# Two half-chunk chains, interleaved, for the feed-forward that runs behind the attention

## What is computed

```python
x = x + attention(layernorm(x), ctx)                 # 16 heads, softmax over 1601 columns
n = layernorm(x)                                     # "t1"
logits = n @ router_w.T                              # "router"
w, top1 = softmax(logits).max(-1), logits.argmax(-1)
x = x + w * (n @ expert_w[top1].T + expert_b[top1])  # "e0".."e15", then the bias, "gb"
n = layernorm(x)                                     # "t2"
a = softmax(where(mask, -1e9, n @ win_k)) * gauss    # "score"
x = x + tanh(concat(a @ ctx, n) @ W_c.T)             # "aT", "z"
n = layernorm(x)                                     # "t3"
h = gelu(n @ w1 + b)                                 # "h"
alpha = softmax_of_top8((h @ w2) / tau)              # "logits", one row of 64 slots per token
slots = (alpha.T @ n) / alpha.sum(0)                 # "slots"; GRU and attention on 64 slots
x = x + alpha @ f(slots)                             # "alphaT", at the very end
```

## The kernel before

| step | before |
| --- | --- |
| turn attention output, y | 10, 12; 15, 17 |
| t1, router | 28, 30; 33 |
| e0 to e15 | 38, 42, 48, 52, 58, 64, 68, 72, 76, 80, 84, 88, 92, 98, 102, 106 |
| gateT; gb | 55; 112, 114 |
| t2, score | 125, 127; 130, 132 |
| aT, z | 145, 147; 150, 158 |
| t3, h, logits, slots, alphaT | 178, 180; 183; 189; 203; 207 |

## Time and profile before

### The profile page before, as it was taken

How to read it: one execution, slowest core, us unless ns; L and a number is a source line. 1 busy time by engine, 2 the same in 40 slices (tenths; PEclk the granted TensorE clock), 3 DMA queues, 4 the chain that set the end, 5 groups by cost and what they waited for, 6 DMA issues and landing times.

```text
span 1084.4 us, 13614 instructions
## 1 busy us (share of the span) xinstructions
PE 978.2 (90%) x4794; PEld 390.6 (36%) x4794; DVE 745.5 (69%) x1704; ACT 571.3 (53%) x1063; POOL 63.8 (6%) x91
## 2 busy tenths in 40 slices
PE   6799999999889999989889989989989999889986
PEld 3453323323333334423323333423333333334643
DVE  4688888887677777776677777776767764235634
ACT  2456766666454456665445546665445547740330
POOL 3441000000000000000000000000000000100000
PEclk9899999999899989999899989999899989999999
DMA  7936500001000000001000000001000000140022
GB/s 187 200 73 111 121 1 15 16 1 35 1 16 1 16 1 14 3 1 55 1 16 1 15 1 13 3 1 54 1 15 1 0 2 1 40 125 2 1 97 78
DMA packets 33931, 36.19 MB, mean 33 GB/s; under 512 B 6670, under 2 KB 30523, under 8 KB 33603
## 3 DMA queue, kind: packets, MB, share of 16 engines
q1 hardware_dynamic: 32542, 34.17, 12.5%
q10 hardware_dynamic: 1242, 0.90, 0.6%
q0 software_dynamic: 80, 0.26, 0.1%
HBM read 21.55 MB, written 7.35 MB: 27 GB/s over the span
## 4 chain that ended last, share of the span: by engine, by line
issue 51%; PE 30%; DVE 9%; DMA 2%; ACT 2%; POOL 2%; DVEq 2%; SPq 1%; POOLq 0%; ACTq 0%
PE ps_m L1064 7%; PE ps_o L1148 7%; PE ps_e L1350 5%; DVE mx L1651 4%; PE ps_e L1022 2%; DMA xres<-in_x 1%; PE ps_m L1350 1%; SPq L545 1%; PE ps_m L1168 1%; PE ps_m L1298 1%; POOL rstd L684 1%; POOL xres L735 1%; PE ps_m L1301 1%; DVE xn L1643 1%; DMA x<-xres 1%
## 5 line engine op out<-in xcount | busy, mean ns | idle before, releaser
L1651 DVE TENSOR_REDUCE mx<-ps_m 128x1 f32<-128x401 f32 x1024 | 538.3, 568 | 198.0 <-PE ps_m L1064 190.6
L848 ACT ACTIVATE probs<-ps_e 128x512 f32<-128x512 f32 (+1 forms) x763 | 437.1, 598 | 342.2 <-PE ps_e L1350 340.5
L1064 PE MATMUL ps_m<-k_stack,q_stack 99*128 99x401 bf16 x1024 | 319.4, 343 | 36.6 <-DVE mx L1651 34.9
L1350 PE MATMUL ps_e<-q_stack,k_stack 101*128 101x512 bf16 (+1 forms) x763 | 299.5, 394 | 10.9 <-ACT probs L848 8.7
L1148 PE MATMUL ps_o<-probs,v_heads 128*32 128x512 f32 (+1 forms) x1664 | 228.9, 623 | 0.0
L1350 PEld LDWEIGHTS ps_e<-q_stack,k_stack 101*128 101x128 bf16 (+1 forms) x763 | 75.9, 100 | 261.8 <-ACT probs L848 167.7
L1064 PEld LDWEIGHTS ps_m<-k_stack,q_stack 99*128 99x128 bf16 x1024 | 102.0, 100 | 183.8 <-DVE mx L1651 131.0
L1252 PE MATMUL ps_m<-expert_w,xnT 128*128 128x512 f32 x192 | 99.4, 598 | 15.2 <-DVE xb L1788 15.2
L1148 PEld LDWEIGHTS ps_o<-probs,v_heads 128*32 128x32 f32 (+1 forms) x1664 | 33.1, 109 | 60.7 <-issue 49.4
L848 ACT ACTIVATE probs<-ps_m 128x512 f32<-128x512 f32 (+1 forms) x69 | 41.6, 603 | 15.2 <-PE ps_m L1350 15.1
L1788 DVE SCALAR_TENSOR_TENSOR xb<-ps_m,hot,xb 128x256 f32<-128x256 f32 x84 | 40.6, 484 | 7.9
(11 more groups left out here) (333 smaller groups left out, 720.0 us busy)
## 6 DMA issues: line engine op xcount, KB each, us to landing
q_stack<-q_parts SPq DMA_DIRECT2D x78, 64.0 KB, 2.6
expert_w<-in_expert_wT SPq DMA_DIRECT2D x2, 1024.0 KB, 12.9
xres<-in_x SPq DMA_DIRECT2D x4, 512.0 KB, 3.8
x<-xres SPq DMA_DIRECT2D x4, 512.0 KB, 3.2
probs<-x SPq DMA_DIRECT2D x1, 2048.0 KB, 8.5
k_stack<-alphaT SPq DMA_DIRECT2D x10, 200.1 KB, 7.6
probs<-in_ctxT SPq DMA_DIRECT2D x3, 512.0 KB, 7.5
q_parts<-probs SPq DMA_DIRECT2D x4, 384.0 KB, 3.0
```

The lines of the kernel that those rows point to most:

```text
L848: act.activation(probs[0:n, k % 2, h, :], score_bank(c, k, h)[0:n, :], ACT.Exp).then_inc(s["exp_done"], 1)
L1064: pe.matmul(ps_m[:, (UNITS * n1 + u) % RING, 0:SPLIT], qst[0:MAX_ROW, g, h, P * t:P * t + P], kst[0:MAX_ROW, HG * g + h, QUARTER_START[q]: ...
L1350: pe.matmul(score_bank(c, k, h)[0:n, :], kst[0:ROWS, HG * g + h, P * st:P * st + n], qst[0:ROWS, g, h, :], start=True, stop=True).then_inc ...
L1651: dve.tensor_reduce(mx[:, q, col:col + 1], ps_m[:, (UNITS * n1 + u) % RING, 0:SPLIT], AX.X, ALU.max)\
```

## The change

Behind chunks 1 to 3, the feed-forward of a chunk runs as two chains, one for tiles 0 and 1, one for tiles 2 and 3. `HALF_STEPS` is placed once for each, with the second chain's first step 6 quarters after the first one's router, and its first expert at least 5 quarters after the first chain's last. Both chains and the row-maxima and output jobs share the same two banks. From the hidden layer on (`h`, `logits`, `slots`, `alphaT`) the chunk stays whole (`choice`). Each engine goes on with three generators in turn in every quarter.

- A job of a half has both 128-row blocks in one bank: `turned_half` writes two k by two tiles, ScalarE takes them with one copy. The number of copies stays 10 a chunk. The weights' transpose goes to `attT`, not `aT`.
- An expert job is the same tile by two experts, but in four products of 256 columns in quarters AT to AT + 3, where it was two of 512.
- Router, gate, softmax and root steps are done by halves: the same element count in twice as many instructions. There are semaphores for each half.
- Normalised tiles are due 1 quarter ahead of the transposes (3 or 4 before); expert jobs of a chain start at least 5 quarters apart (4 before).
- `z` starts with the products that don't need the transposed weights.
- The last chunk's feed-forward keeps its order and uses the same functions, run through `at_once`; so its experts too are in 256 columns.

```diff
-JOBS = [("ota", None, 10, 3), ("otb", "ota", 2, 3), ("y0", "otb", 3, 3), ("y1", "y0", 2, 3), ("t1a", "y1", 11, 3),
-        ("t1b", "t1a", 2, 3), ("router", "t1b", 3, 2), ("e0", "router", 5, 6)]
-JOBS += [(f"e{i}", f"e{i - 1}", 4, 6) for i in range(1, 4)] + [("gateT", "e3", 3, 3), ("e4", "gateT", 1, 6)]
...
+HALF_STEPS = [("ot", None, 10, 3), ("y", "ot", 3, 3), ("t1", "y", 8, 3), ("router", "t1", 3, 2), ("e0", "router", 5, 6),
+              ("e1", "e0", 5, 6), ("gateT", "e1", 2, 3)]
+HALF_STEPS += [(f"e{i}", f"e{i - 1}", 5, 6) for i in range(2, NE // 2)]
+HALF_STEPS += [("gb", f"e{NE // 2 - 1}", 4, 4), ("t2", "gb", 9, 3), ("score", "t2", 3, 3), ("aT", "score", 9, 3), ("z", "aT", 3, 9), ("t3", "z", 15, 3)]
+LAST_STEPS = [("h", "t3", 3, 5), ("logits", "h", 6, 2), ("slots", "logits", 14, 6), ("alphaT", "slots", 4, 3)]
...
+        if name == "ot" and h:
+            return at.get(("router", 0), NEVER) + 6
+        if name == "e0" and h:
+            return max(at.get((f"e{NE // 2 - 1}", 0), NEVER) + 5, at.get((after, h), NEVER) + lag)
...
+def go_on(works, quarter):
+
+    for work in works:
+        while work[1] <= quarter:
+            work[1] = next(work[0], NEVER)
...
-                    for k in range(KT):
-                        yield AT[name] + 2 * k
-                        mm = pe.matmul(bank(name, c), xnT[:, k, P * t:P * t + P], expert_w[:, k, CT * j:CT * j + CT],
-                                       start=(k == 0), stop=(k == KT - 1))
...
+                for e in range(2):
+                    for k in range(KT):
+                        if e or k:
+                            yield AT[f"e{i}", h] + 2 * e + k
+                        mm = pe.matmul(half_bank(f"e{i}", c, h)[:, D * e:D * e + D], xnT[:, k, tok:tok + P],
+                                       expert_w[:, k, CT * j + D * e:CT * j + D * e + D], start=(k == 0), stop=(k == KT - 1))
...
-                yield AT["t1a"] - 4
-                normal(xa, NC + 3 * c + 1)
...
+                yield AT["t1", h] - 1
+                normal_half(xa, 0, c, h)
...
+                work = [begin(steps) for steps in (behind(c - 1, 0), behind(c - 1, 1), choice(c - 1))] if c else []
```

More of the change, by code:

```diff
@@ L193, in begin, with at_once @@
     return [steps, next(steps)]
-def go_on(work, quarter):
-    while work and work[1] <= quarter:
-        work[1] = next(work[0], NEVER)
+def go_on(works, quarter):
+    for work in works:
+        while work[1] <= quarter:
+            work[1] = next(work[0], NEVER)
+def at_once(steps):
+    for _ in steps:
+        pass
 JOB = job_numbers()
@@ L730, in _, with rsqrt_half @@
             pool.wait_ge(s["hb_ready"], 1)
-            def behind(c):
+            def rsqrt_half(i, c, h):
+                pool.wait_ge(var_half[h], 3 * c + i + 1)
+                pool.tensor_tensor(var_e[:, tiles(h)], mv[:, tiles(h), 1], eps[:, tiles(h)], ALU.add)
+                pool.drain()
+                pool.tensor_tensor(rstd[:, tiles(h)], var_e[:, tiles(h)], neg_half[:, tiles(h)], ALU.pow).then_inc(rstd_half[h], 1)
+            for c in range(NC):
                 pool.wait_ge(s["x_loaded"], 16 * (c + 1))
@@ L886, in behind, with window_exp @@
+            def window_exp(c, h):
+                act.wait_ge(negmax_half[h], c + 1)
+                act.activation(tail[:, tiles(h)], st4[:, 0, tiles(h)], ACT.Exp, bias=neg_big[:, 0:1])
+                for t in range(HT * h, HT * h + HT):
                     last = act.activation(work2[:, t, :], work[:, t, :], ACT.Exp, bias=st4[:, 0, t:t + 1],
                                           accum_out=rowsum[:, t:t + 1])
-                last.then_inc(s["rowsum_ready"], 1)
-                yield AT["aTa"] + 2
@@ new lines, in norm_turned, with rows_half @@
+            def norm_turned(i, c, h):
+                pe.wait_ge(xn_half[h], 3 * c + i + 1)
+                yield from turned_half(f"t{i + 1}", c, h, xn)
+            def rows_half(name, c, h, after, rows, weights):
+                wait_half_taken(pe, after, c, h)
+                half_free(pe, name, c, h)
+                for t in range(HT):
+                    if t:
+                        yield AT[name, h] + t
+                    for k in range(KT):
+                        mm = pe.matmul(half_bank(name, c, h)[:, D * t:D * t + D], rows[:, k, HC * h + P * t:HC * h + P * t + P],
+                                       weights[:, k, :], start=(k == 0), stop=(k == KT - 1))
+                fills_half(mm, name, c, h)
@@ L1219, in behind @@
+            def behind(c, h):
+                yield AT["ot", h]
+                if c == 0 and h == 0:
                     pe.wait_ge(s["ld_fill"], N_FILL)
@@ new lines, in behind @@
+                router_half(c, h)
+                for i in range(NE // 2):
+                    yield AT[f"e{i}", h]
+                    yield from expert_half(i, c, h)
+                    if i == 1:
+                        yield AT["gateT", h]
+                        gates_half(c, h)
+                yield AT["gb", h]
+                yield from bias_half(c, h)
+                yield AT["t2", h]
+                yield from norm_turned(1, c, h)
+                yield AT["score", h]
+                yield from rows_half("score", c, h, "t2", xnT, win_k)
@@ L1740, in behind @@
[L1740 to L1755 removed]
+                last.then_inc(var_half[h], 1)
@@ L1822, in behind @@
[L1822 to L1830 removed]
+                last.then_inc(a_half[h], 1)
```

951 lines of the change are left out of this document (396 added, 555 removed).

## The result

The changed kernel takes 1119.03 us, median of 4 runs (1117.1 to 1124.97), against 1087.07 (1086.31 to 1095.68) for the kernel before on the same chip: ratio 1.0285, 95% interval 1.0219 to 1.0351. That is slower by 32 us, outside the predicted range. The profiled execution took 1120.59 us, its span is 1118.5 (1084.4 before).

The account below looks back on a forecast made before the run. PE was taken as the limit only in the steady experts, with waits and half clock elsewhere. Chunks 1 and 2 -1.6 each, chunk 3 -1, tail +0.6: -3.6 against 1086.4, so 1083 us; range 1058 to 1108.

Parts of the forecast that it names:

- Balance of the engines: Chunks 1 and 2: moving norms and softmaxes beside the other half's experts gains 3.3 us a chunk; chunk 3 gains 1.
- Waits of one quarter, bank: PE at the shared banks: ten tight starts on DVE steps, 8.4 us against 5.6 before, +2.8 a chunk.
- Waits of one quarter, tiles: Normalised tiles due 1 quarter ahead instead of 4: PE waits for DVE, +1.5 us a chunk (0 to +5).
- Waits on ACT's copies: Copies between turn and y, t1 and router, t2 and score wait twice, about 0.45 us each: +1.4 a chunk.
- The clock: PE's half-clock falls at first norm, router and bias products go: 4 us a chunk saved (0 to 6.8).
- five called bare: Starts at quarters 35, 41, 53, 86, 123, no product or values before on PE: 6.4 us in all.
- five called covered: The other five tight starts, with a product or the values before them on PE: 0.4 us each, 2.0 together.
- Experts in 256 columns: Expert jobs in 256-column products: 0 behind the attention, 0.6 us more after the last score (2.2 at most).
- The residual: VectorE needs the next residual at quarter 15: 2 us of cover, cost 0; without it up to 2 us.
- The signs named ahead: Profile after: 241 us a chunk, clock 0.98 to 0.99; wrong if bank waits exceed 12 us or clock stays 0.96.
- chains that block each other on the two banks: Rival: all ten waits bare, ACT and norm at upper range, no clock gain: +8 a chunk, 1110 us; chance 0.19.
- More half clock: Rival: six further falls of 3.4 us a chunk at half clock, 10 us, 1113 us; chance 0.04.

Follow-up runs that it names:

- a longer hold: Changed kernel, with each expert job of a half holding its bank 7 quarters instead of 6: 1087.5 us, ratio 0.9985.
- VectorE's new order: Changed kernel, with VectorE doing the feed-forward's steps ahead of each quarter's maxima instead of after them: 1071.0 us, ratio 0.9809.
- the interleaved kernel with all edits: Changed kernel with feed-forward steps ahead of maxima, expert takes one quarter earlier, tiles due two quarters ahead, two 512-column expert products: 1057.0 us, ratio 0.9730.
- both edits on the kernel before: Kernel before, with VectorE's feed-forward steps ahead of the quarter's maxima and its expert takes one quarter earlier: 1061.8 us, ratio 0.9750.

## Why the prediction was wrong

The forecast was 1083 us, a gain of 3.6; it lost 32 to 34. Its terms for chunk 1, each beside what PE's idle times of 0.3 us and more in the timeline, or its busy time, come to:

| term | forecast | measured |
| --- | --- | --- |
| Balance of the engines | -3.3 | waits for maxima 9.3 to 4.7: -4.6 |
| Waits of one quarter, bank | +2.8 | 5.6 to 14.0: +8.4 |
| Waits of one quarter, tiles | +1.5 | 0 to 4.1: +4.1 |
| Waits on ACT's copies | +1.4 | all waits for ACT 2.1 to 3.6: +1.5 |
| The clock | -4 | busy time 222.6 to 223.6: +1.0 |
| waits put down to issue | none | 1.9 to 0.5: -1.4 |
| sum | -1.6 | +9.0 (the chunk: +9.6) |

The forecast took its price for a copy, 0.45 us, from a wait that the profile puts down to issue; so the rows of ACT and of issue belong together, and come to +0.1 where +1.4 was forecast.

**Waits of one quarter: the step that failed.** The mechanism was named, with its sign and nearly all its places: the ten counted starts are 11.1 us of PE's waiting, where I had 8.4. The five called bare cost 5.5 (6.4 forecast); the five called covered cost 5.6, where I took 0.4 each, 2.0. The cover was misread. At 59 and 75 I counted value products of the same quarter, but these stand behind the feed-forward's piece in PE's queue (322.94 is the expert product of quarter 59; its value products start at 323.57), and so they hide nothing: 59 waits 1.61. At 118 PE did have a product of 0.45 before it, and VectorE had 2.25 us of work between that and the take's end (1.04, 0.73 and 0.48): it waits 2.17. Two things were not priced at all. The price of 1.28 came from a kernel with one chain, where the take has only its own quarter's maxima ahead of it; with two chains, tiles or another job's take join the queue. And the start at 47 has the maxima's own `mrow` step between itself and its bank: 2.90 us, the longest of all, was in no count. For the tiles, "half of it falls in slots already counted" was wrong; each of the three waits of 0.76, 1.45 and 1.93 is PE's own idle time. The runs show these waits to be the main cost. The change adds 33.4 us to chunks 1 to 3, of which 25.8 are idle time of PE; earlier takes, a longer hold and VectorE's new order take 19.3, 27.0 and 35.0 us of idle time out again, of gains of 19.4, 31.6 and 47.1 in these chunks. For earlier tiles this holds only in part (3.1 of 11.1).

**The clock.** The forecast said that three of the falls would go. Those at the first norm and at the router did; after the first half's bias products one is left (at 342.2, for 3.4 us), and one at the logits (471.9). Two others came in the place of those that went. That makes four falls of 3.4 us, 13.6 at half clock for about 17, in chunk 1, and yet PE's busy time there didn't fall. Busy time by stretch in chunk 1 of the changed kernel, the clock third from the end:

```profile
302.00:308.40 6.40, 3.50 (x22) 1.45 (x21) 4.35 (x11) 1.84 (x4) 0.00 (x0) 1.00 0.01 1
308.40:320.00 11.60, 10.74 (x63) 5.92 (x63) 7.54 (x21) 6.44 (x13) 0.00 (x0) 1.00 0.14 36
396.80:400.30 3.50, 1.33 (x8) 0.75 (x7) 2.98 (x7) 0.67 (x2) 0.00 (x0) 1.00 0.00 0
400.30:403.70 3.40, 3.40 (x15) 1.20 (x13) 0.58 (x1) 0.60 (x1) 0.00 (x0) 0.50 0.00 0
454.50:458.30 3.80, 1.51 (x8) 0.58 (x7) 3.68 (x10) 1.43 (x3) 0.89 (x2) 1.00 0.00 0
458.30:461.70 3.40, 3.40 (x14) 0.95 (x13) 0.57 (x1) 0.60 (x1) 0.00 (x0) 0.50 0.00 0
```

Half clock begins at 400.3 and 458.3, in each case within 0.8 us after a long wait of PE has ended (2.17 and 1.93 us). In chunk 3 it begins at 966.9, in a wait of PE for ScalarE's `hT`, and lasts 13.7 us; PE's busy time there grows by 5.1 us (212.75 for 207.63), and its idle time by 9.3, near the 8.5 and 7.9 of the other two chunks; together 14.4. After the wait of 2.90 that ends at 306.44 the clock stays at 1.00, so a wait isn't enough by itself. The mean clock of the profiled execution is 0.969 for 0.968, and nothing of the term of -12 us is left. I had argued from the four bank waits of the kernel before that such waits leave the clock alone. The Trainium skill (TensorE: Matmul & The Clock Gate, A second HAM failure mode: psum-queue depth-cycling) says that short idles between groups of matmuls, from going round PSUM banks, can bring the clock down repeatedly. By these traces that is so at most in part: falls follow some of the new waits, and with nearly all of them gone in the interleaved kernel with all edits the mean clock is 0.987; but in the changed kernel the total at half clock didn't rise above that of before, and with waits taken out in other ways the clock is 0.974 (takes and tiles earlier), 0.966 (hold of seven) and 0.967 (both edits on the kernel before). So the cause of the falls stays open.

**Right or nearly so.** Experts in 256 columns cost nothing behind the attention: 1121.5 us with two products again, 1119.0 without; in the kernel before they even gained. The Trainium skill's rule on the spacing of a stream (TensorE: Matmul & The Clock Gate, Back-to-back issue gap), which the prediction read as speaking against halved columns, shows no cost here. After the last score 128 instructions of 256 columns fill 29.2 us, as 64 of 512 columns did (29.0), though the busy time of their weight loads went from 11.7 to 23.8 us, and the tail grew by 0.3 where I had 0.6:

```profile
L1247 PE MATMUL ps_m<-expert_w,xnT 128*128 128x256 f32 x128 | 29.2, 382 | 1.3 <-DVE xb L1731 1.3
```

VectorE's busy time in chunk 1 is 177.9 us (178 to 179 forecast), 1.5 more than before, so the added small instructions were priced nearly right (2.3). The residual is no wait: in chunks 1 and 2 the profile lists waits of VectorE for maxima alone.

```profile
DVE mx L1598 <- PE ps_m L1073: 130.8, 142, 3.6
```

Whether the balance gain is there isn't shown. The waits for maxima fell to 4.7 where about 7 was forecast, but a PE that waits elsewhere gives VectorE time to catch up: in the interleaved kernel with all edits they are 7.2 again, against 8.4 in the whole-chunk kernel with both, and the interleaved one is idle no less. So at most 1.2 us of the 3.3 a chunk is seen.

**The signs named ahead.** Chunk 1 takes 252.6 us for 241, and the waits on the banks are 14, where the forecast was to be wrong from 12; the clock, 0.97 and 0.98 in chunks 1 and 2 and 0.95 in chunk 3, was to be 0.98 to 0.99. Of the rivals, the one whose mechanism the runs show is that of the chains that block each other on the two banks: +8 a chunk, 1110 us, with a chance of 0.19. (More half clock, 1113 us, is nearer in number, but the span is at half clock no longer than before.) It was short by 9 us: 3 in chunks 1 and 2, which took +9.6 and +9.4, and 6.4 in chunk 3, of which 5.1 are PE's busy time at the lower clock. Its sum isn't consistent either: with the upper ends that the prediction itself gives, +1.4 for ACT and +5 for the tiles, it comes to +10.3 a chunk and 1117 us, and the -3 for all starts covered should be -1.6 at the prediction's 0.4 each.

## What to carry to other kernels

When two in-order queues hand work to each other on a fixed schedule, walk both queues item by item at each handover that is due in the very next step. What stands before the awaited instruction (here VectorE's take) makes the wait longer; only what stands before the waiting one (here PE's next job on the bank) is cover. A second interleaved chain multiplies such handovers and lengthens the queue in front of each of them, so look first at the order within a step and at one step more of slack. Here those two, without any interleaving, were worth 2.5%, and the kernel before had needed them too.

## What the runs showed of the hardware

Not expected was how many of VectorE's 0.57 us reductions can be put off at no price: with all of them behind the feed-forward's steps, PE's waits for maxima in chunk 1 stayed at 4.5 us (4.7 before the edit), and in the kernel before at 9.3; with takes and tiles earlier as well they are 7.2. Halving the columns of 32 fp32 products a chunk to 256 gained 9 us in the kernel before, with PE idle as long and the clock higher in chunks 1 and 2, and the runs don't say why. And half clock began within 0.8 us after idle times of PE of 2.17 and 1.93 us, but not after one of 2.90.
